# State-space block of a decoder megakernel: the products of du and B made by ScalarE with tokens on partitions and turned into the banks that the scans read, with a shorter convolution and norm

## The reference, cut to what matters

```python
def _ssm_forward(hidden_states, z, in_proj_w, conv_w, conv_b, x_proj_w, dt_proj_w, dt_proj_b, A_log, D):
    x = jnp.einsum('ed,bld->bel', in_proj_w, hidden_states)
    xp = jnp.pad(x, ((0, 0), (0, 0), (DC - 1, 0)))
    xc = jax.lax.conv_general_dilated(xp, conv_w[:, None, :], ..., feature_group_count=DI)
    u = jax.nn.silu(xc + conv_b[None, :, None])
    x_dbl = jnp.einsum('ke,bel->bkl', x_proj_w, u)
    dt_lo, Bm, Cm = x_dbl[:, :DR], x_dbl[:, DR:DR + DS], x_dbl[:, DR + DS:]
    delta = jax.nn.softplus(jnp.einsum('er,brl->bel', dt_proj_w, dt_lo) + dt_proj_b[None, :, None])
    A = -jnp.exp(A_log)
    def step(state, xs):                       # over the 256 tokens
        d_t, B_t, C_t, u_t = xs
        dA = jnp.exp(d_t[..., None] * A)
        state = state * dA + (d_t * u_t)[..., None] * B_t[:, None, :]
        return state, jnp.einsum('ben,bn->be', state, C_t)
    ...
    y = y + D[None, :, None] * u
    return jnp.swapaxes(y * jax.nn.silu(z), 1, 2)
x = x + _L0_xattn_ref(ctx_1024, _layernorm(x), ...)      # the second argument is z
```

## Time and profile before

| | |
|---|---|
| three runs of the kernel | 2175.06, 2167.53, 2173.30 us; median 2173.3 |
| the profiled execution: its time | 2174.94 us |
| the profiled execution: its span | 2172.9 us |
| PE, DVE, ACT, POOL busy | 86%, 57%, 36%, 12% of the span |
| mean granted clock of PE | 0.921 of full speed |
| the changed stage in the span | 138.8 to 328.3 us |

### The profile page before, as it was taken

One profiled execution on the slowest core, in us unless ns is written; L12 is line 12 of the kernel. 1 busy time (PEld: TensorE's weight loads), 2 busy tenths in 40 slices (PEclk: granted clock), 3 DMA queues, 4 the chain that ended last, 5 costly groups with the idle time before them and its releaser, 6 DMA issues.

```text
span 2172.9 us, 25396 instructions
## 1 busy us (share of the span) xinstructions
PE 1871.0 (86%) x9009; PEld 1192.1 (55%) x9014; DVE 1246.5 (57%) x2842; ACT 791.9 (36%) x1871; POOL 252.0 (12%) x241
## 2 busy tenths in 40 slices
PE   7875667898578699999899498999998999998698
PEld 3641223655455466666566364555555677777355
DVE  7658998654753555555584773333334666665221
ACT  4325445115432233333445122333333555553111
POOL 5210000010114100000110200000001222220111
PEclk9797887999779899999999799999999999998899
DMA  3010000000461200000100303000002000002210
GB/s 145 1 58 0 1 0 21 29 1 2 198 228 61 82 1 1 1 1 1 39 1 1 156 1 135 1 1 0 1 1 118 1 1 1 1 1 112 71 34 13
DMA packets 17387, 82.73 MB, mean 38 GB/s; under 512 B 3152, under 2 KB 10068, under 8 KB 13040
## 3 DMA queue, kind: packets, MB, share of 16 engines
q1 hardware_dynamic: 11184, 70.96, 8.3%
q0 software_dynamic: 2944, 8.03, 1.2%
q10 hardware_dynamic: 3136, 2.13, 0.3%
HBM read 72.84 MB, written 8.81 MB: 38 GB/s over the span
## 4 chain that ended last, share of the span: by engine, by line
PE 74%; DVE 16%; issue 5%; ACT 3%; POOL 1%; DMA 1%; POOLq 0%; another core or an unknown queue 0%; DVEq 0%; ACTq 0%; SPq 0%
PE bank L136 60%; PE bank L141 9%; PE bank L3690 4%; DVE space L925 2%; PE bank L3712 2%; DVE space L914 2%; DVE space L1498 1%; DVE space L3192 1%; DVE space L174 1%; DVE space L268 0%; DVE space L185 0%; DVE space L2540 0%; POOL space L2776 0%; DVE x L2089 0%; POOLq L4200 0%
## 5 line engine op out<-in xcount | busy, mean ns | idle before, releaser
L136 PE MATMUL bank<-space 128*128 128x256 f32 (+14 forms) x6729 | 1449.7, 419 | 72.4 <-ACT space L952 10.3
L136 PEld LDWEIGHTS bank<-space 128*128 128x128 f32 (+6 forms) x6734 | 886.3, 179 | 587.9 <-issue 389.2
L141 PE MATMUL bank<-consts,space 128*128 128x128 f32 (+1 forms) x1602 | 253.8, 300 | 149.0 <-DVE space L185 49.6
L141 PEld LDWEIGHTS bank<-consts,space 128*128 128x128 f32 (+1 forms) x1602 | 202.2, 153 | 214.1 <-issue 114.9
L136 PE MATMUL bank<-space,consts 128*128 128x512 f32 (+2 forms) x150 | 92.3, 742 | 60.9 <-DVE space L920 51.4
L193 POOL TENSOR_TENSOR space<-space,consts 128x4 f32<-128x4 f32 x20 | 22.6, 1131 | 702.2 <-DVE space L180 702.2
L2571 ACT ACTIVATE space<-bank,space 128x256 f32<-128x256 f32 x128 | 59.5, 470 | 95.7 <-DVE space L2525 95.7
L2776 POOL TENSOR_TENSOR space<-space,consts 128x4 f32<-128x4 f32 x64 | 68.6, 1071 | 220.7 <-DVE space L2707 220.7
L2525 DVE TENSOR_REDUCE space<-bank 128x2 f32<-128x512 f32 x64 | 44.1, 688 | 86.9 <-PE bank L136 86.8
L136 PEld LDWEIGHTS bank<-space,consts 128*128 128x128 f32 (+1 forms) x150 | 29.0, 218 | 105.1 <-DVE space L920 72.8
L2699 DVE TENSOR_REDUCE space<-bank 128x2 f32<-128x512 f32 x64 | 44.2, 691 | 71.1 <-PE bank L136 71.1
(11 more groups left out here) (369 smaller groups left out, 1954.3 us busy)
## 6 DMA issues: line engine op xcount, KB each, us to landing
space<-in_L_ffn SPq DMA_DIRECT2D x13, 2048.0 KB, 11.8
space<-in_L_attn SPq DMA_DIRECT2D x9, 2048.0 KB, 11.8
space<-in_L_xattn SPq DMA_DIRECT2D x4, 2048.0 KB, 9.5
expert_results<-space SPq DMA_DIRECT2D x16, 128.0 KB, 3.4
space<-expert_results SPq DMA_DIRECT2D x8, 256.0 KB, 4.5
space<-in_L_xattn SPq DMA_DIRECT2D x1, 1919.0 KB, 18.3
space<-in_L_xattn SPq DMA_DIRECT2D x1, 1536.0 KB, 6.2
space<-in_L_attn SPq DMA_DIRECT2D x1, 1344.0 KB, 14.2
```

The costliest lines, as they stand in the source:

```text
L136: return self.nc.tensor.matmul(out, lhsT, rhs, start=first, stop=last, skip_group_check=True)
L141: return self.nc.tensor.transpose(out, src, eye)
```

## The change

In the loop, DVE no longer multiplies du by B, and B is no longer spread over the partitions. In place of these:

- B is also made with tokens on partitions (`bT`: 16 more matmuls of 16 columns in the opening), and du is turned once to tokens on partitions (`duT`: 16 transposes in the opening, copied out by ACT and DVE).
- For each state n and half g, ACT makes du * B as four activations of 128x256, Copy with the column of `bT` as its scale (`weigh_b`, into two buffers `dbT`).
- PE turns these back, four transposes of 128x128 for each half of a unit (`make_b`), into the banks 4, 5 and 6 in turn, and DVE's scan reads its second operand from the bank. The scan is in two halves of 512.
- The rows of C are spread one half at a time through bank 7 (`spread_half`, `c_half`).

In the opening, `CUTS` runs with g outside; the first tap of the convolution is made by ACT (Identity with scale and bias) and the whole convolution of the fourth piece by PE (`project_convolved`, with weights that POOL makes at L1109); the halves of softplus follow each other; a small Exp brings the table of Exp in ahead. The norm no longer writes its rows: ACT applies it inside Silu, by a scale and a bias per token. The stage's weights lose half of `select` and gain `taps`.

```diff
-    CUTS = [(f, g) for f in range(DC) for g in range(NG)]
+    CUTS = [(f, g) for g in range(NG) for f in range(DC)]
...
     def tensor(self, e):
...
+        self.project_convolved(e)
         for g in range(NG):
+            e.wait_ge(*s.activated(2 * g + 2))
...
+        for i in range(NT):
+            for k in range(DC):
+                done = c.mm(bk[6][:, i * SSM_N:(i + 1) * SSM_N], self.u[:, k, i * P:(i + 1) * P],
+                            w["x_proj"][:, k, 0:SSM_N], k == 0, k == DC - 1)
+        done.then_inc(*s.bT_mm.one)
+        for g in range(NG):
+            self.spread_half(e, 0, g)
...
         for t in range(N + 2):
+            if t < N:
+                for g in range(NG):
+                    self.make_b(e, t, g)
             if t >= 2:
...
                 for g in range(NG):
                     done = c.mm(bk[2 * f + g], c.ident, self.db[u % 4][:, cut(g)], n == 0, n == SSM_N - 1)
                 done.then_inc(*s.summed.one)
...
+            if t < N:
+                n, f = self.UNITS[t]
+                if n + 1 < SSM_N:
+                    self.spread_half(e, n + 1, f)
...
+    def make_b(self, e, u, g):
...
+        n, f = self.UNITS[u]
+        h = 2 * u + g
+        e.wait_ge(*s.b_weighed(2 * n + g + 1))
+        if h >= 3:
+            e.wait_ge(*s.scanned(h - 2))
+        for i in range(4):
+            done = c.turn(c.banks[4 + h % 3][:, i * P:(i + 1) * P], self.dbT[n % 2][:, 4 * g + i, f * P:(f + 1) * P])
+        done.then_inc(*s.b_made.one)
...
     def vector(self, e):
...
-                nc.vector.tensor_tensor(self.db[t % 4], self.du[:, f, :], self.bc[n % 3], ALU.mult).then_inc(*c.v.next())
+                for g in range(NG):
+                    h = 2 * t + g
+                    e.wait_ge(*s.b_made(h + 1))
+                    nc.vector.tensor_tensor_scan(self.db[t % 4][:, cut(g)], self.da[t % 3][:, cut(g)], bk[4 + h % 3], 0.0,
+                                                 ALU.mult, ALU.add).then_inc(*s.scanned.one)
             if t >= 1:
...
+                nc.vector.tensor_tensor(y, y, self.cc[n % 3], ALU.mult).then_inc(*s.weighted.one)
-            if t < N:
...
-                nc.vector.tensor_tensor_scan(h, da, h, 0.0, ALU.mult, ALU.add).then_inc(*s.scanned.one)
...
     def scalar(self, e):
...
+        for u, (n, f) in enumerate(self.UNITS):
+            if u + 1 < N:
+                self.decay(e, u + 1)
+            if n + 1 < SSM_N:
+                self.weigh_b(e, n + 1, f)
+                self.c_half(e, n + 1, f)
...
+    def weigh_b(self, e, n, g):
...
+        if n >= 2:
+            e.wait_ge(*s.b_made(4 * n - 4))
+        for i in range(4 * g, 4 * g + 4):
+            done = c.nc.scalar.activation(self.dbT[n % 2][:, i, :], self.duT[:, i, :], ACT.Copy,
+                                          scale=self.bT[:, i, n:n + 1])
+        done.then_inc(*s.b_weighed.one)
```

More of the change, by code:

```diff
@@ L904, in vector @@
                                     ALU.mult).then_inc(*s.du_ready.one)
-        e.wait_ge(*s.du_ready.all)
+        e.wait_ge(*s.inverse.all)
+        nc.vector.scalar_tensor_tensor(out=self.n[:, 2, :], in0=self.mv[:, :, 0], scalar=-1.0, in1=self.n[:, 1, :],
+                                       op0=ALU.mult, op1=ALU.mult).then_inc(*s.shifted.one)
+        for half in range(2):
+            e.wait_ge(*s.du_turned(3 + half))
+            nc.vector.tensor_copy(flat(self.duT[:, 4 + 2 * half:6 + 2 * half, :]), bk[2 + half]).then_inc(*s.du_by_vector.one)
         N = len(self.UNITS)
@@ L977, in scalar @@
             nc.scalar.activation(tmp, tmp, ACT.Ln, bias=1.0).then_inc(*s.logs.one)
[L979 to L993 removed]
+        nc.scalar.activation(self.loaded[:, 0:1], c.ident[:, 0:1], ACT.Exp)
+        for g in range(NG):
+            self.c_half(e, 0, g)
+        for half in range(2):
+            e.wait_ge(*s.du_turned(half + 1))
+            nc.scalar.activation(flat(self.duT[:, 2 * half:2 * half + 2, :]), bk[half], ACT.Copy).then_inc(*s.du_by_scalar.one)
+        e.wait_ge(*s.bT_out.all)
+        e.wait_ge(*s.du_by_scalar.all)
+        self.weigh_b(e, 0, 0)
         e.wait_ge(*s.firsts.all)
@@ L996, in scalar @@
         e.wait_ge(*s.du_ready.all)
+        self.decay(e, 0)
+        e.wait_ge(*s.du_by_vector.all)
+        self.weigh_b(e, 0, 1)
+        N = len(self.UNITS)
         for u, (n, f) in enumerate(self.UNITS):
-            if u >= 3:
-                e.wait_ge(*s.scanned(u - 2))
-            nc.scalar.activation(self.da[u % 3].rearrange("p (b s) -> p b s", s=S)[:, :, 1:],
-                                 self.delta[:, f, :].rearrange("p (b s) -> p b s", s=S)[:, :, 1:], ACT.Exp,
-                                 scale=self.a[:, f, n:n + 1]).then_inc(*s.decays.one)
@@ L1003, in scalar @@
-            if f == 0:
-                c_out(n)
-            elif n + 1 < SSM_N:
-                b_out(n + 1)
-        e.wait_ge(*self.norm.s.normed.all)
-        for t in range(8):
-            b, f = divmod(t, DC)
-            z = self.z[:, TPB * b + f, :]
-            nc.scalar.activation(z, z, ACT.Silu).then_inc(*s.z_silu.one)
+            if u + 1 < N:
[3 more added lines that the diff above has]
+                self.c_half(e, n + 1, f)
@@ new lines, in scalar @@
+        e.wait_ge(*s.shifted.all)
+        for i in range(NT):
+            nc.scalar.activation(self.z[:, i, :], c.x[:, i, :], ACT.Silu, bias=self.n[:, 2, i:i + 1],
+                                 scale=self.n[:, 1, i:i + 1]).then_inc(*s.z_silu.one)
+    def weigh_b(self, e, n, g):
+        c, s = self.c, self.s
+        if n >= 2:
[4 more added lines that the diff above has]
+        done.then_inc(*s.b_weighed.one)
@@ new lines, in decay, with c_half @@
+    def decay(self, e, u):
+        c, s = self.c, self.s
+        n, f = self.UNITS[u]
+        if u >= 3:
+            e.wait_ge(*s.scanned(2 * u - 4))
+        by_batch = lambda ap: ap.rearrange("p (b s) -> p b s", s=S)[:, :, 1:]
+        c.nc.scalar.activation(by_batch(self.da[u % 3]), by_batch(self.delta[:, f, :]), ACT.Exp,
+                               scale=self.a[:, f, n:n + 1]).then_inc(*s.decays.one)
+    def c_half(self, e, n, g):
+        c, s = self.c, self.s
+        if n >= 3:
+            e.wait_ge(*s.weighted(2 * (n - 3) + 2))
+        e.wait_ge(*s.c_spread(2 * n + g + 1))
+        c.nc.scalar.activation(self.cc[n % 3][:, g * HALF:(g + 1) * HALF], c.banks[7], ACT.Copy).then_inc(*s.c_out.one)
@@ L1016, in gpsimd @@
         cut = lambda g: slice(g * HALF, (g + 1) * HALF)
-        self.norm.gpsimd(e)
+        f = self.CUTS[3][0]
+        e.wait_ge(*self.ld.all)
+        nc.gpsimd.tensor_tensor(self.tapped, self.w["taps"].rearrange("p (a b) -> p a b", b=P),
+                                repeat(self.w["in_proj"][:, 0, f * P:(f + 1) * P], 4), ALU.mult).then_inc(*s.tapped.one)
         for g in range(NG):
```

175 lines of the change are left out of this document (100 added, 75 removed).

## The result

| | before | after |
|---|---|---|
| median of the runs beside each other | 2174.14 us (4 runs) | 2135.75 us (4 runs, 2129.54 to 2142.64) |
| ratio, with its 95% interval | | 0.9835 [0.981, 0.9859] |
| the profiled execution: time, span | 2174.94, 2172.9 us | 2142.64, 2140.5 us |
| the changed stage in the span | 138.77 to 328.28 us | 137.15 to 293.90 us |
| its length | 189.51 us | 156.75 us |

The time fell by 38 us between medians and by 32.3 us between the two profiled executions. The stage itself is 32.8 us shorter.

The account below looks back on a forecast made before the run. DVE, busy throughout the loop at 4.45 us a unit, was taken as the bound. Loop -33.2, opening -2.8 and cold start +3.5 gave -32.5 us: 2174.94 to 2142.4 us profiled, 2141 for the median, range 2131 to 2158.

Parts of the forecast that it names:

- The loop, -33.2: Block's loop: 31 steps at 3.38 us a unit instead of 4.45, with DVE still the bound, save 33.2 us.
- The bank as source, 0: Half scans reading one operand from a PSUM bank cost nothing more than from SBUF; nothing added.
- The opening, -2.8: Before the loop: the first unit's scan comes 2.8 us earlier in all, with -6 and +4 as ends.
- free at about 163.4: Opening: DVE finishes the thin matmuls' copy and the norm's statistics at about 163.4, so delta starts 5.0 us earlier.
- the serial list that I laid behind 168.8: Opening, after delta and du: transposes, copy, activations, decay, transposes in series, giving the first half scan at 172.0.
- The cold start, +3.5: Loop's start: PE enters at half clock, units with a sum cost 5.9 us instead of 3.38; 3.5 taken, ends 0 and 8.
- The end, 0: Stage's end: sum, L928 to L941, stays 10.3 us from the last weighting; no change.
- (a): Loop: another limit between 3.4 and 3.8 us a unit, the gain falling by 9 us to 2150; 14%.
- (b): Loop: PE stays at half clock, 5.9 us a unit, and the kernel is slower at 2216 us; 5%.
- (c): Opening: it grows by 4 us or more, giving 2148; 4%.
- (d): Behind the block: the gain is hidden because something waits for other work, such as a DMA; no change; 2%.

Follow-up runs that it names:

- e0: The changed kernel once more, unaltered: 2138.9 us, ratio 0.9855 to the kernel before; stage 156.67 us.
- e1: The changed kernel's new loop with the old opening and norm: 2137.56 us, ratio 0.9848 to the kernel before; stage 159.19 us.
- e5: Changed kernel plus one more ACT activation of 128x256 per unit, into a buffer nobody reads: stage 160.07 us against 156.75.
- e4: Changed kernel with each transpose of the loop done twice, 16 per unit: stage 167.40 us, unit 3.68 us.
- e3: Changed kernel with half scans reading delta in SBUF instead of the bank: stage 156.96 us against 156.75; 2149.64 us in one run.
- e2: The changed kernel's new opening with the old loop: 2164.14 us, ratio 0.9978 to the kernel before; stage 180.56 us.
- e7: Changed kernel with norm statistics ahead of softplus and the copy of bT behind du's second piece: 2134.06 us, ratio 0.9837; stage 153.05 us.
- e8: e7 with eight transposes of B's rows, copied by DVE, in place of 32 thin matmuls: 2143.26 us, ratio 0.984; stage 152.86 us.
- e9: e8 with unit 30 weighted before the scans of unit 31: 2138.33 us, ratio 0.9841; stage 152.80 us.
- e6: Changed kernel with transposes doubled and sums of states 1 to 14 cut to 16 columns: stage 161.25 us.

## Why the prediction was right, and where its steps failed

The forecast was 2141 us for the median, 2142.4 for the profiled execution. Measured were 2135.75 and 2142.64. Both lie in the stated range, 2131 to 2158. That the second agrees to 0.2 us is luck in large part: the loop, which is the mechanism and nearly all of the gain, is right to 0.7 us, but the opening and the cold start are each wrong by 3.3 us, and in opposite directions. The median lies 5.2 us below the forecast; taken once more (e0) the changed kernel lay 31.4 us below the kernel beside it, so part of that is scatter too.

- **The loop, -33.2.** Right. 31 steps of 3.358 instead of 4.453 us save 33.9. The half scan was taken at 1.135 us and paces at 1.12; L914's place is empty and nothing took it. e1, the loop alone, gives 30.3 with the old opening and what the new work costs in it. ACT, foreseen at 3.1 to 3.4 us a unit, is at 3.1 (e5). PE, foreseen at 3.2, is at 2.8 (e4).
- **The bank as source, 0.** Right, shown by e3: 1200 ns from a bank, 1204 from SBUF. The Trainium skill (VectorE: DVE Perf Modes, the TRN2 errata) would have made the stage 4.1 us longer in the changed kernel than in e3, as an estimate from its cycles; e3's was 0.2 us longer. For this instruction the measurement decides against that figure.
- **The opening, -2.8.** Wrong: the first unit's scan ends 40.42 us after the stage's start, before it was 39.92, so +0.5. The step that failed is "free at about 163.4", 24.6 us after the start. It stood between the thin matmuls at full clock and those at half. They ran at half to the last, 6.93 us, and began 1.0 us later than I put them, so delta came at 28.1 us. e5's opening, with the clock falling 2.9 us later, has delta at 25.5: PE's granted clock makes 2.65 of the 3.5 us that this step was off. What was ahead of it (Silu, Abs) came within 0.3 us of what I had worked out. Behind it 12.3 us passed from delta to the scan's end, forecast 12.5, but with an error in the working: the serial list that I laid behind 168.8 adds up to 5.25 us and so to 174, not to 172.0. The 172.0 fits only if the transposes start when the first two pieces of du are done, as they did (168.05, 2.8 us after delta). e2 and e7 show what held delta at all: where the statistics don't stand behind the thin matmuls, it starts at 22.0.
- **The cold start, +3.5.** Wrong for this kernel: it cost 0.2 us, because the clock rose 1.7 us before the first sum. Where the loop starts earlier, the first sum meets half clock: 1.36 us are paid in e7, 1.2 to 1.6 in e8 and e9 and 1.8 in e5; how much depends on when the clock changes. Even then it is at most about half of what I took: one sum alone is hit, that of unit 0, behind which the transposes for unit 3 wait in PE's queue.
- **The end, 0.** Short by 0.45 us. I followed the order of DVE and not what stands in PE's queue: unit 30 is now weighted after the last scan, so its four sums stand ahead of the last four (x8 in 3.70 us, before 2.08 us of waiting, now 2.66).

Summed up: -33.9 + 0.5 + 0.2 + 0.45 = -32.8 us, as the stage shows. The terms are worked out from the same trace: from the end of the first unit's scan to the end of the last 103.20 us (138.03 before), and from there to the end of the stage 13.13 (11.56 before); one weighting of 1.12 us has moved from the first of these stretches to the second.

**The rivals.** (a), another limit at 3.4 to 3.8 us, did not come, though there was little room: e5 reaches 3.5 us with one activation of 0.4 us more per unit, e4 3.68 with eight transposes more. (b), half clock throughout, did not come: the clock stayed at 1.00 from 179.74 to 288.96. The rule that I set beside it (the Trainium skill, TensorE: Matmul & The Clock Gate, Part 4 on PE-mode transpose, by which transposes do not count as busy in the same way) is not borne out here. The clock rose at 573.97 in the kernel before with 32 transposes and nothing else on PE, in the changed kernel at 179.74 behind 3.4 us of twelve transposes and two spread halves without a sum, and in e6 it stayed full with 46.7 of PE's 62.53 busy us spent on transposes. (The rows call them MATMUL and don't say whether they run in the mode that the Trainium skill means; each is one row, where an fp32 matmul of `c.mm` is two.), the transposes at half clock, are no evidence for the rule either: those at 55.8 us in the kernel before stayed at half, and the same sixteen in the changed kernel, from 56.65 us on, ended with the clock rising at 60.27. (c), an opening 4 us or more longer than before, did not come: it was 0.5 us longer, which is 3.3 us worse than forecast. (d), a gain that other work hides, did not come: the kernel is shorter by what the stage is shorter.

## What to carry to other kernels

When an engine is full and the others wait for it, moving one of its instructions elsewhere pays the pace of that instruction, as long as the others' real work, not the sum of their rows, stays under the new unit; doubling a piece of their work measures that room. Where a change has two parts, look at the point where they meet: here a new batch of thin matmuls stood ahead of the statistics that the other part had moved, and of a gain of 9 us 6.5 were lost; moving the statistics and one copy (e7) gave 3.7 of them back. Taking away a wait pays only up to the next one in the queue: e8 put 1.0 us of PE's work in the place of 6.9 and gained 0.2, since a copy on another engine held the same place. And a forecast that leans on the granted clock in a short stretch can be off by the moment at which it changes: the same opening had delta 2.65 us earlier in one execution (e5) than in another.

## What the runs showed of the hardware that I had not expected

- An engine's busy time overstates its load, though overlapped time counts once in it: a transpose's row lasts 272 ns and the next starts 0.11 us after it, an activation of 128x256 lasts 497 ns and the next starts 0.40 us after it, and where idle time follows, the row still counts whole. PE was busy 3.08 us a unit and had work for 2.81 (e4), ACT 3.22 and 3.1 (e5).
- Transposes alone raise the granted clock: in the kernel before it rose at 573.97 with only transposes on PE since 569.94 and 8.17 us of idle time ahead of them, and in the changed kernel at 292.38 behind twelve (289.25 on, 3.61 us of idle time ahead). It stayed at 1.00 in e6 with PE busy 78% of the time, mostly with them.
- The thin matmuls (128x16, fp32) took 0.2 us a row at half clock with PE busy without a gap for 6.9 us, and the clock did not rise in that stretch (154.40 to 161.30). Why it rose behind the transposes and not behind these was not tried.
